# Scores, row maximum and exponentials of an attention head handed on in two parts of the keys

## The reference

```python
q = (x @ Wq).reshape(b, n, HEADS, DIM) * DIM ** (-0.5)
kv_scores, indices = _pk(x, Wq_pk, pk_keys)          # two top-16 lists, their 256 sums, top 16 of these, softmax
ind = indices + offsets[None, None, :, None]
k = jnp.einsum('bnhk,bnhkd->bnhd', kv_scores, keys_table[ind])
v = jnp.einsum('bnhk,bnhkd->bnhd', kv_scores, values_table[ind])
sim = jnp.einsum('bihd,bjhd->bhij', q, k)
sim = jnp.where(causal, sim, neg)
attn = jax.nn.softmax(sim, axis=-1)
out = jnp.einsum('bhij,bjhd->bhid', attn, v)
...
return out @ Wo
```

## Time and profile before

| what | value |
|---|---|
| time, three runs | 3163.86 us median (3163.5 to 3173.11) |
| profiled execution | 3170.45 us, its span 3168.7 us |
| PE busy | 2133.7 us (67%), mean granted clock 0.813 |
| DVE busy | 1764.0 us (56%) |
| ACT busy | 1038.7 us (33%) |
| POOL busy | 1993.4 us (63%), all but 7.5 us of it the 2048 gathers |

### The profile page before, as it was taken

One profiled execution on the slowest core, in us unless ns is written; L12 is line 12 of the kernel. 1 busy time (PEld: TensorE's weight loads), 2 busy tenths in 40 slices (PEclk: granted clock), 3 DMA queues, 4 the chain that ended last, 5 costly groups with the idle time before them and its releaser, 6 DMA issues.

```text
span 3168.7 us, 41159 instructions
## 1 busy us (share of the span) xinstructions
PE 2133.7 (67%) x13440; PEld 1420.2 (45%) x13498; DVE 1764.0 (56%) x6187; ACT 1038.7 (33%) x1971; POOL 1993.4 (63%) x2075
## 2 busy tenths in 40 slices
PE   5255565657565667676777778686878776774768
PEld 3134343434343444453554546454646554443333
DVE  3636564746565656566565747565656655336441
ACT  3133232323232324233333434242434322323333
POOL 0056777777777777777777777767776777770000
PEclk8667686868687979788888879798989888886889
DMA  2023434343434344444444443434343434353200
GB/s 59 16 81 105 134 111 137 112 136 114 136 114 137 112 134 117 122 126 125 126 124 128 123 124 104 139 101 137 102 122 100 118 110 118 115 173 102 76 17 7
DMA packets 172565, 348.15 MB, mean 110 GB/s; under 512 B 38816, under 2 KB 93760, under 8 KB 170176
## 3 DMA queue, kind: packets, MB, share of 16 engines
q0 software_dynamic: 98304, 268.57, 29.4%
q1 hardware_dynamic: 71408, 71.71, 7.1%
q10 hardware_dynamic: 2640, 5.24, 0.5%
HBM read 333.83 MB, written 11.53 MB: 109 GB/s over the span
## 4 chain that ended last, share of the span: by engine, by line
POOL 36%; PE 24%; DVE 16%; issue 14%; ACT 6%; DMA 2%; DVEq 2%; SPq 0%; ACTq 0%; POOLq 0%
POOL ring L736 36%; PE acc L815 7%; PE wide L924 3%; PE turn L806 3%; DVE kv L1307 2%; DMA ring<-in_kv_table,idxT 2%; PE acc L406 2%; PE rowsum L787 1%; PE wide L868 1%; PE wide L440 1%; DVE att_m L1335 1%; ACT att_p L1087 1%; ACT pt_sb L1032 1%; PE wide L867 1%; DVE pos L1378 1%
## 5 line engine op out<-in xcount | busy, mean ns | idle before, releaser
L736 POOL DMA_INDIRECT ring<-in_kv_table,idxT x2048 | 1985.9, 970 | 854.6 <-issue 607.8
L815 PE MATMUL acc<-kv,pt_sb 128*128 128x128 f32 x3968 | 597.5, 304 | 116.6 <-ACT pt_sb L1032 116.1
L787 PE MATMUL rowsum<-ring,w_block 128*32 128x256 f32 x4096 | 349.3, 443 | 405.0 <-DMA ring<-in_kv_table,idxT 399.8
L815 PEld LDWEIGHTS acc<-kv,pt_sb 128*128 128x128 f32 x3968 | 541.4, 213 | 163.3 <-ACT pt_sb L1032 163.3
L1032 ACT ACTIVATE pt_sb<-turn 128x512 f32<-128x512 f32 (+3 forms) x544 | 291.2, 558 | 349.9 <-PE turn L806 348.2
L787 PEld LDWEIGHTS rowsum<-ring,w_block 128*32 128x32 f32 x4096 | 101.1, 116 | 615.7 <-DMA ring<-in_kv_table,idxT 452.0
L924 PE MATMUL wide<-kv,qT 128*128 128x512 f32 (+3 forms) x576 | 267.5, 599 | 108.0 <-DVE gs L1307 83.4
L1335 DVE TENSOR_REDUCE att_m<-wide 128x1 f32<-128x128 f32 (+14 forms) x120 | 147.0, 1225 | 182.9 <-PE wide L924 177.5
L1307 DVE CUSTOM_DVE_ANT_0 kv<-wide,att_p 128x2048 f32<-128x2048 f32 x56 | 128.3, 2291 | 213.5 <-ACT att_p L1087 209.1
L806 PE MATMUL turn<-ident,att_p 128*128 128x128 f32 x960 | 163.2, 306 | 84.6 <-ACT kv L1049 70.8
L924 PEld LDWEIGHTS wide<-kv,qT 128*128 128x128 f32 x576 | 112.1, 212 | 239.4 <-issue 238.5
(11 more groups left out here) (245 smaller groups left out, 3079.0 us busy)
## 6 DMA issues: line engine op xcount, KB each, us to landing
ring<-in_kv_table,idxT POOLq DMA_INDIRECT x2048
kv<-in_adj SPq DMA_DIRECT2D x27, 1024.0 KB, 5.3
wq_pair<-in_Wq SPq DMA_DIRECT2D x64, 128.0 KB
v_dram<-sums_sb SPq DMA_DIRECT2D x128, 64.0 KB
kv<-v_dram SPq DMA_DIRECT2D x16, 512.0 KB
att_p<-in_Wo SPq DMA_DIRECT2D x16, 512.0 KB, 5.4
kv<-in_adj ACTq DMA_DIRECT2D x5, 1024.0 KB, 7.8
x_dram<-x SPq DMA_DIRECT2D x17, 64.0 KB, 1.9
```

The lines of the kernel that those rows point to most:

```text
L736: pool.indirect_dma_start(ring[:, slot, i, :], None, kv_table, bass.IndirectOffsetOnAxis(idxT[:, r % 2, u:u + 1], 0))\
L787: mm = pe.matmul(rowsum[32 * k:32 * k + 32, 0:ROW], w_block[:, at:at + 32], ring[:, slot, k, :], start=(tk == 0), stop=(tk == 3))
L815: mm = pe.matmul(dst, pt_sb[:, q % 2, b * P:(b + 1) * P], rhs(4 * q + b), start=(q + b == 0), stop=(q == len(widths) - 1 and b == widths[q ...
```

## The change

For query tiles of nine and more blocks of 128 keys (more than two chunks), a head's scores are handed on in two parts: the first two chunks (1024 keys) and the rest (128 to 896 keys). For fewer blocks there is one part, as before.

- `scores_of`: `s_made` is incremented after each part. The second head's scores wait for `p_made` part by part: its first part starts when the first part's exponentials of the first head are made, its second part when the second part's are.
- `row_max`: a maximum over each part, each behind its own `s_made`, into two columns of `own_r`; a drain; the maximum of the two; then the negative as before.
- `exps`: still behind `s_max` of the whole row, two exponentials, each with a row sum of its own in the new tile `att_part` and its own increment of `p_made`.
- `own`: for a tile whose main part had two parts, one addition of the two row sums with a drain ahead of what was there.
- The turning of the second head's `att_p` still waits for both parts.

```diff
+    HALF = 2
+
+    def parts(n):
+
+        widths = chunk_widths(n)
+        return [widths[:HALF], widths[HALF:]] if len(widths) > HALF else [widths]
...
+    def parts_before(n, h):
+        return parts_to[n] + h * len(parts(n))
...
                     def scores_of(h):
-                        for c, w in enumerate(widths):
-                            mm = pe.matmul(wide[:, c * 512:c * 512 + w * P], qT[:, h, :],
-                                           kv[:, 4 * c:4 * c + w, h * P:(h + 1) * P], start=True, stop=True)
-                        mm.then_inc(s_made, 1)
+
+                        for i, part in enumerate(parts(q)):
+                            if h % 2:
+                                pe.wait_ge(p_made, parts_before(q, h - 1) + i + 1)
+                            for c in range(HALF * i, HALF * i + len(part)):
+                                w = widths[c]
+                                mm = pe.matmul(wide[:, c * 512:c * 512 + w * P], qT[:, h, :],
+                                               kv[:, 4 * c:4 * c + w, h * P:(h + 1) * P], start=True, stop=True)
+                            mm.then_inc(s_made, 1)
...
-                    pe.wait_ge(p_made, met(q, 2 * s) + 1)
                     scores_of(2 * s + 1)
...
-                    pe.wait_ge(p_made, met(q, 2 * s) + 2)
+                    pe.wait_ge(p_made, parts_before(q, 2 * s + 2))
                     values_of(2 * s + 1).then_inc(o_made, 1)
...
-                    act.activation(att_p[:, 0:q * P], wide[:, 0:q * P], ACT.Exp, bias=att_nm[:, h:h + 1],
-                                   accum_out=att_sum[:, h:h + 1]).then_inc(p_made, 1)
+                    for i, part in enumerate(parts(q)):
+                        lo, hi = 512 * HALF * i, 512 * HALF * i + P * sum(part)
+                        act.activation(att_p[:, lo:hi], wide[:, lo:hi], ACT.Exp, bias=att_nm[:, h:h + 1],
+                                       accum_out=att_part[:, i, h:h + 1]).then_inc(p_made, 1)
...
             def row_max(q, h):
-                dve.wait_ge(s_made, met(q, h) + 1)
-                dve.reduce_max(att_m[:, h:h + 1], wide[:, 0:q * P], AX)
+                if len(parts(q)) == 1:
+                    dve.wait_ge(s_made, parts_before(q, h) + 1)
+                    dve.reduce_max(att_m[:, h:h + 1], wide[:, 0:q * P], AX)
+                else:
+                    for i, part in enumerate(parts(q)):
+                        lo, hi = 512 * HALF * i, 512 * HALF * i + P * sum(part)
+                        dve.wait_ge(s_made, parts_before(q, h) + i + 1)
+                        dve.reduce_max(own_r[:, i:i + 1], wide[:, lo:hi], AX)
+                    dve.drain()
+                    dve.tensor_tensor(att_m[:, h:h + 1], own_r[:, 0:1], own_r[:, 1:2], ALU.max)
                 dve.drain()
                 dve.tensor_scalar(att_nm[:, h:h + 1], att_m[:, h:h + 1], -1.0, None, ALU.mult).then_inc(s_max, 1)
...
                 if d > 0:
-                    dve.tensor_tensor(att_sum[:, :], att_sum[:, :], own_a[:, :], ALU.mult)
+                    if len(parts(d)) == 2:
+                        dve.tensor_tensor(att_sum[:, :], att_part[:, 0, :], att_part[:, 1, :], ALU.add)
+                        dve.drain()
+                        dve.tensor_tensor(att_sum[:, :], att_sum[:, :], own_a[:, :], ALU.mult)
+                    else:
+                        dve.tensor_tensor(att_sum[:, :], att_part[:, 0, :], own_a[:, :], ALU.mult)
```

More of the change, by code:

```diff
@@ L115, in chunks_of @@
         return chunks_before(heads // H + 1, heads % H)
+    HALF = 2
+    def parts(n):
+        widths = chunk_widths(n)
+        return [widths[:HALF], widths[HALF:]] if len(widths) > HALF else [widths]
+    parts_to = [0, 0]
+    for n in range(1, T + 1):
+        parts_to.append(parts_to[-1] + H * len(parts(n)))
+    def parts_before(n, h):
+        return parts_to[n] + h * len(parts(n))
     def met(n, h):
@@ L202, in build_network @@
         att_sum = sb("att_sum", [P, H])
+        att_part = sb("att_part", [P, 2, H])
         own_m = sb("own_m", [P, H])
```

## The result

The changed kernel takes 3160.69 us (median of 20 runs, 3153.98 to 3168.39), the kernel before in the same rounds 3170.27 us (20 runs, 3161.24 to 3177.97): ratio 0.9974 (95% interval 0.9964 to 0.9983), 8.3 us less (5.4 to 11.4). That is 0.26%, inside the 0.3% to which the prediction gave 0.70. The side was right, and the sum less than half of what came.

What follows compares the result with a forecast made beforehand. POOL's gathers were taken to bound the kernel, savings counting only where POOL stalls on PE (42 us, tiles 9 to 15). Per-step gains minus 0.26 us, times deciding steps, net 3.8 us: 3163.86 - 3.8 = 3160.1 us, range 3150 to 3171.

Steps and rivals of the forecast that it cites:

- Prices of one step: First head's scores and maximum: gain min(d, 1.22) - 0.35 us, d = 0.216 us per block of keys beyond eight.
- The second activation: Splitting the exponentials on ACT costs 0.26 us, a loss in every step; bounds 0.15 and 0.48.
- The second head's maximum: On DVE it grows by 0.35 us, covered by 1.67 us of slack ahead of ACT; effect nothing.
- Rival C: DVE's first maximum does not proceed beside PE; every step loses 0.61 us, 12.2 us in all, 3176.1 us; chance 0.10.
- D: DVE, ahead of time, waits for `sum_head`; only the exponentials' price is left, 5.2 us, 3169.1 us; chance 0.13.
- B: Scores, maximum and exponentials of both heads are the chain; POOL's stalls vanish, 42 us, 3121.9 us; chance 0.04.
- rival A: Second parts of the scores fall into PE's 1.2 GHz stretches, so more maximum is hidden; 9.4 us, 3154.5 us; chance 0.17.
- the prediction's counts of steps: Steps deciding POOL's stalls on PE, read from one profile: three in tile 11, four in 12, four in 13.
- Tile 15: One deciding step gains 0.87 + 0.7 - 0.26 = +1.3 us; POOL's waits on PE fall from 3.6 to 2.3.
- the hand-on: Tile 15's second-head scores start when the first 1024 columns are made, 0.7 us earlier; nothing in tile 14.
- Tile 14: Gain of +0.61 us a step over two deciding steps, 1.2 us won.
- Tiles 9 and 10: Tile 9 loses 0.39 us a step, 1.2 us in all; tile 10 loses 0.18 a step, 0.5 us.

Runs made afterwards that it cites:

- max_only: The changed kernel with only scores and maximum in two parts, exponentials one activation again; ratio to the kernel before 0.9965, 11.1 us less.
- exps_only: The changed kernel with only exponentials and their hand-on in two parts, one maximum over the whole row; ratio to the kernel before 1.0023, 7.3 us more.
- only_15: The kernel before with the whole change, maximum and exponentials of both heads, in tile 15 alone; ratio to the kernel before 0.9994.
- before_again: The kernel before, unchanged, run a second time under a name of its own; ratio 0.9996.
- first_max_13: Against the kernel before: first head's maximum in two parts in tiles 11 to 13, whole change in tile 15, tile 14 as before; ratio 0.9953.
- first_max: Against the kernel before: first head's maximum alone split in tiles 11 to 14, whole change in tile 15; ratio 0.9939, the second time 0.9955.
- early_only: The kernel before with the change in tiles 9 to 13 alone; ratio to the kernel before 0.9970, 9.5 us less.
- both_max: Against the kernel before: both heads' maxima split in tiles 11 to 14, exponentials whole there, whole change in tile 15; within 3153 to 3155 us.
- late_only: The kernel before with the change in tiles 14 and 15 alone; ratio to the kernel before 0.9982, 5.7 us less.
- after_again: The changed kernel, unchanged, run a second time under a name of its own; ratio to the kernel before 0.9971.

## Why the prediction was right and wrong

**Prices of one step: right.** Up to the negated maximum, steps at 2.4 GHz gained 0.13 us in tile 10, 0.35 in 11, 0.56 in 12, 0.78 in 13 and 0.83 in 14, and lost 0.07 in tile 9. The forecast was 0.08, 0.30, 0.51, 0.73, 0.87 and a loss of 0.13. What is added is 0.30 us, not 0.35: back to back, two maxima of 1024 and 640 columns take 1.96 us, 0.08 less than the 1.22 and 0.82 that the rows gave for each. The second activation was put at 0.26 us; from start to PE it is 2.03 against 1.79. The second head's maximum is hidden, as said. Rival C is out (the maximum runs beside PE: 1.96 us for both), D is out (of 20 such rows in tiles 9 to 13 one waits for PE, 0.30 us, in tile 11), B is out.

**The clock of the first head's scores: the mis-sized term.** The prediction took the length of the second part, 0.216 us a block, from a step at 2.4 GHz, and kept the slow step of the earlier trace rows for rival A, as if all steps were one or all the other. They are mixed. In tiles 11 to 13 of the five kernels with a whole maximum, 28 of 60 first heads started slow, in the eight with a split one 45 of 96, 47% both times, but not alike by tile: 9, 13 and 6 of 20, then 10, 14 and 21 of 32. In most slow steps of tiles 11 and 12 the second part takes PE longer and hides more of the first maximum: in the mean, slow steps went from 5.95 to 5.19 us in tile 11 and from 6.24 to 5.48 in 12, 0.76 us each, where the prediction had argued that the slow stretch is mostly over by then. In tile 13 it mostly is: slow steps went from 6.67 to 5.88, hardly more than the 0.78 of steps at 2.4 GHz. With half of the steps slow the gain per step is about 0.55 in tile 11 and 0.66 in 12, instead of 0.30 and 0.51. So A was not a rival but the state of about half the steps. With the prediction's counts of steps (three, four and four) and 0.25 us for the exponentials, tiles 11, 12 and 13 give 0.9 + 1.6 + 2.1 = 4.6 us, where it had 3.0. The stalls of the two pairs of profiles show more, some 11 us (from 31.1 to 20.2 in the mean); part of that is which steps happened to be slow (in tiles 11 and 12, 6 of 16 in the two profiles of the changed kernel and 10 of 16 in those before; in tile 13, where the change has more slow steps, this works against it).

**Tile 15: right as far as it went, too small.** The forecast was 1.3 us, POOL's whole stall of 2.4 went. The prediction had the hand-on, not what it does to PE's clock. In the kernel before the exponentials and the second head's scores start so, on ACT:

```profile
2724.97 1.86 ACT L1141 ACTIVATE att_p<-wide,att_nm 128x1920 f32<-128x1920 f32 x1 [1.93 <-DVE att_nm L1337]
```

and in the changed kernel, ACT and PE:

```profile
2717.14 1.11 ACT L1162 ACTIVATE att_p<-wide,att_nm 128x1024 f32<-128x1024 f32 x1 [1.10 <-DVE att_nm L1366]
```

```profile
2718.49 3.46 PE L944 MATMUL wide<-kv,qT 128*128 128x512 f32 x8 [2.87 <-ACT att_p L1162]
```

From the exponentials to the scores it was 2.09 us and is 1.35, the 0.7 forecast. But PE, idle for 2.87 us instead of 4.45, goes on at 2.4 GHz; the same scores take 3.46 us instead of 5.16. The granted clock of these scores, in two windows before and one after:

```profile
2727.10:2729.50 2.40, 2.40 (x3) 0.99 (x4) 0.00 (x0) 0.00 (x0) 1.79 (x3) 0.52 0.36 109
2729.50:2732.20 2.70, 2.70 (x10) 1.00 (x12) 0.00 (x0) 0.00 (x0) 2.09 (x3) 0.80 0.35 99
```

```profile
2718.50:2721.90 3.40, 3.40 (x12) 1.42 (x12) 1.22 (x1) 0.83 (x2) 2.51 (x3) 1.00 0.33 94
```

The step shrinks from 29.09 to 26.33 us: 0.56 up to the first exponentials (the first head's own scores were 0.26 slower in this profile), 0.74 from the hand-on, 1.70 from the clock, less 0.24 for the second activation. One part alone does not do it: the step takes 30.04 us in `max_only`, 29.03 in `exps_only`, 26.45 in `only_15`. Of the 2.76 us POOL can use the 2.4 that it had stood still. The scores behind this wait take 3.46 us in all eight profiles with both parts in tile 15 and more than 5.1 us in the five others.

**Tile 14: 1.2 us forecast, and a loss came.** POOL stalls 5.8 us there in both profiles of the changed kernel, 2.9 us more than before. Step 0 takes 29.62, 29.61 and 29.61 us in the kernel before, `before_again` and `only_15`, 32.53 in the changed kernel. Its first head's scores start at 1.2 GHz there and not in those three, but that is not all: with the maximum whole, a slow start cost 2.1 us (31.70 in `first_max_13`). Nor is it the second activation: `first_max` has the exponentials whole there and stalls 5.7 us, as does `early_only`, in which tile 14 is as before and step 0 starts slow (32.05 us). Later in the step PE computes the second head's scores and comes back for the first head's values, in the kernel before and in the changed one:

```profile
2558.71 4.94 PE L924 MATMUL wide<-kv,qT 128*128 128x512 f32 x8 [4.21 <-ACT att_p L1141]
...
2568.19 1.16 PE L815 MATMUL acc<-kv,pt_sb 128*128 128x128 f32 x8 [2.52 <-ACT pt_sb L1032]
2569.19 0.60 PE L806 MATMUL turn<-ident,att_p 128*128 128x128 f32 x4
```

```profile
2547.88 3.25 PE L944 MATMUL wide<-kv,qT 128*128 128x512 f32 x8 [2.73 <-ACT att_p L1162]
...
2558.00 2.08 PE L830 MATMUL acc<-kv,pt_sb 128*128 128x128 f32 x8 [4.86 <-ACT pt_sb L1051]
2559.87 1.06 PE L821 MATMUL turn<-ident,att_p 128*128 128x128 f32 x4
```

The granted clock of the values' stretch, before and after:

```profile
2568.20:2571.00 2.80, 2.80 (x25) 2.80 (x26) 2.57 (x6) 1.09 (x3) 2.19 (x3) 1.00 0.43 130
```

```profile
2558.00:2562.00 4.00, 4.00 (x18) 4.00 (x19) 3.63 (x9) 1.03 (x2) 3.09 (x4) 0.50 0.43 124
```

As in tile 15 the second head's scores, here behind a wait of 2.73 us instead of 4.21, run faster. But here the copies of the first head's chunks stand behind the picks on ACT, so PE, done earlier, waits 4.86 us instead of 2.52, and the values run at half the clock: from the picks' exponentials to the second head's on ACT it takes 6.42 us (2556.96 to 2563.38) instead of 4.07 (2567.15 to 2571.22). The same exchange stands in step 0 of tile 14 of eleven of the thirteen profiles: where the second head's scores took 3.25 us (the changed kernel twice, `first_max` twice, `max_only`, `exps_only`), the second head's exponentials came 4.0 to 4.3 us behind their bias; where they took 4.9 to 5.6 us (the kernel before twice, `only_15`, `first_max_13`, `both_max`), 1.6 to 1.9 us. `late_only` and `early_only` do not fit: scores of 4.79 and 4.94 us, and exponentials 3.1 us behind their bias. So that the early scores bring about the loss is argued from rows, and not shown by a run of its own. The prediction had asked what is late next when the scores come early, and not what a longer wait does to PE. Where PE stayed fast, the term is there: step 0 of `both_max` takes 28.78 us, 0.83 less than before, and tile 14 stalls 0.3 us.

**Tiles 9 and 10.** Tile 9 stalls 2.6 and 2.7 us against 0.4 and 0.0, twice the 1.2 that was forecast. But `only_15` stalls 2.1 us there without any change in that tile, and `early_only`, which has the change, 0.0. Tile 10 was to lose 0.5 us and stalled less in both profiles; `only_15` stalls 1.5 there, again without any change. So neither forecast is confirmed or refuted.

**The sum.** The parts came out at 11.1 won (8.3 by the terms) and 7.3 lost (5.2), so the whole rests on a difference of two terms that are each larger than it. POOL's stalls, in the mean of the two profiles of each kernel, change by +2.4 us in tile 9, -2.0 in tile 10, -10.9 in tiles 11 to 13, +2.9 in tile 14 and -2.2 in tile 15, together 9.7 us less; the forecast had +1.2, +0.5, -3.0, -1.2 and -1.3. The surplus is thus in tiles 11 to 13 and, where no forecast is settled, tile 10; in tiles 11 to 13 alone the fall is more than the 4.6 us that the terms give with slow steps counted in. For `first_max` the same count gives 1.7 + 2.6 + 3.1 + 2.4 = 9.8 us against 14 and 19 measured.

The steps show where it is. Means in us over steps 0 to 2, first of the four kernels with the code of before in these tiles (`before`, `before_again`, `late_only`, `only_15`), then of the three with that of the change (`after`, `after_again`, `early_only`); a step goes from its first head's scores to those of the next:

```
            step             to the negated maximum   behind it
tile 11     32.74  31.91     5.41  4.38               27.34  27.54
tile 12     33.41  32.47     5.58  4.75               27.83  27.72
tile 13     34.24  33.51     5.60  4.94               28.64  28.57
```

A step is 0.83, 0.94 and 0.73 us shorter, where the prediction had 0.04, 0.25 and 0.47. The maximum wins 1.03, 0.83 and 0.67 us, instead of 0.30, 0.51 and 0.73; in tile 11 that is more than a step of either speed gains, because 8 of 12 steps were slow before and 3 of 9 after. Behind it 0.26 us a step was to be lost, and in the mean 0.20 is lost, then 0.11 and 0.06 won: the second activation's price, plain in single steps, is covered by differences of about 1 us with PE's clock (step 2 of tile 13 has 28.49 us in one profile of the kernel before and 29.41 in the other). So the term that was sized too small is the first head's gain in tiles 11 and 12. Which part of this the change does by moving slow steps, and which part is chance, stays open.

## What to carry to other kernels

Where a wait is cut in parts, price each part by itself and keep only those whose row is on the chain that decides: here the first head's maximum in tiles 11 to 13 and the whole in tile 15 give some 15 us, and with the rest of the change some 9 are left. Where an engine's clock falls in some steps, count the steps of each kind over several profiles, by tile, before and after, and price a change at both speeds. Work that is handed on earlier to an engine which then waits longer may come back at half its clock.

## What was unexpected of the hardware

The clock of a burst on PE cannot be told from PE's rows just ahead of it. In the changed kernel PE's work ahead of the first head's scores at 2400.04 and at 2433.44 is the same row for row over the last 16 us, down to the last one, followed by the same 2.18 us of waiting; one burst takes 3.03 us, the other 4.73:

```profile
2396.79 1.07 PE L802 MATMUL rowsum<-ring,w_block 128*32 128x256 f32 x16
```

```profile
2430.20 1.07 PE L802 MATMUL rowsum<-ring,w_block 128*32 128x256 f32 x16
```

The Trainium skill, TensorE: Matmul & The Clock Gate, section Part 1: The HAM clock gate, says that where the clock changes varies between runs of one kernel. The two profiles of the changed kernel agree, with slow first heads in other steps of tiles 11 to 13; those of the kernel before differ so in tiles 11 and 12, but have the same slow step in tile 13. The same page of the Trainium skill, section HAM oscillation, says that a wait between bursts can bring the lower clock back in every round; here waits of 4.45 and 4.86 us ended at 0.52 and 0.50, waits of 2.52 and 2.87 us at 1.00, and one of 2.18 us at either. The length of the wait alone does not decide: in step 0 of tile 14 a wait of 2.74 us in `late_only` ended at 0.50, and one of 3.57 us in `exps_only` at 1.00. With 1.7 us for each slow burst of tile 13, this may also be a source of the scatter of 8 us either way among runs of one kernel, which was not tested; it is not the only one, as the stretch behind the last gather differs by some 4 us (319 and 324 us) between the two profiles of the changed kernel.
